# Expert routing stage of a two-layer transformer kernel: the expert choice ahead of the rows' low halves, and a ring of five PSUM banks for gate and up products

## The reference

```python
    def _L0_ffn_ref(x, gate_w, w_up, w_down, sg_gate, sg_up, sg_down):
        ...
        logits = xf @ gate_w.T
        topk_logits, topk_idx = jax.lax.top_k(logits, TOP_K)
        topk_w = jax.nn.softmax(topk_logits.astype(jnp.float32), axis=-1).astype(x.dtype)
        comb = jnp.zeros((N, E), x.dtype).at[jnp.arange(N)[:, None], topk_idx].add(topk_w)
        ...
        for e in range(E):
            g = xf @ wg[e].T
            u = xf @ wu[e].T
            y = jax.nn.silu(g) * u @ w_down[e].T
            out = out + comb[:, e:e + 1] * y
        shared = jax.nn.silu(xf @ sg_gate.T) * (xf @ sg_up.T) @ sg_down.T
        return (shared + out).reshape(b, t, d)
    ...
    x = x + _L0_ffn_ref(_layernorm(x, axis=-1), L0_ffn_gate_w, ...)
```

## Time and profile before

| | us |
|---|---|
| median of 3 runs | 2417.37 |
| lowest, highest | 2417.35, 2419.74 |
| the profiled execution, its own time | 2425.1 |
| its span in the profile | 2423.4 |
| TensorE matmul busy | 2185.1 (90%) |
| VectorE busy | 1776.7 (73%) |
| ScalarE busy | 1664.1 (69%) |
| GpSimd busy | 1076.6 (44%) |

### The profile page before, as it was taken

One profiled execution on the slowest core, in us unless ns is written; L12 is line 12 of the kernel. 1 busy time (PEld: TensorE's weight loads), 2 busy tenths in 40 slices (PEclk: granted clock), 3 DMA queues, 4 the chain that ended last, 5 costly groups with the idle time before them and its releaser, 6 DMA issues. The chain is left out here.

```text
span 2423.4 us, 85735 instructions
## 1 busy us (share of the span) xinstructions
PE 2185.1 (90%) x31693; PEld 1375.4 (57%) x31693; DVE 1776.7 (73%) x5603; ACT 1664.1 (69%) x3894; POOL 1076.6 (44%) x1374
## 2 busy tenths in 40 slices
PE   6979999999967788879999995996999999999766
PEld 4643444444435676768888884563455555555354
DVE  5538999999838677744454444984999999999298
ACT  6955899899843555424454443893799999999644
POOL 3533666666654566636666664562000000000076
PEclk9987999999979899989999998997899999999888
DMA  6552333333232566745553344874232222322242
GB/s 220 203 189 75 93 91 94 94 94 93 65 97 87 146 181 185 171 115 128 141 139 96 93 89 127 267 274 147 65 80 79 81 75 81 82 74 69 64 155 95
DMA packets 363746, 290.45 MB, mean 120 GB/s; under 512 B 228400, under 2 KB 296752, under 8 KB 363344
## 3 DMA queue, kind: packets, MB, share of 16 engines
q1 hardware_dynamic: 349616, 248.24, 37.0%
q0 software_dynamic: 12960, 35.60, 4.7%
q10 hardware_dynamic: 768, 1.12, 0.2%
HBM read 133.53 MB, written 123.69 MB: 106 GB/s over the span
## 5 line engine op out<-in xcount | busy, mean ns | idle before, releaser
L765 ACT ACTIVATE a_pr<-a_pst 128x384 f32<-128x384 f32 (+3 forms) x2176 | 909.2, 486 | 112.6 <-PE a_pst L804 87.3
L804 PE MATMUL a_psc<-a_ke,a_qe 52*64 52x192 f16 (+4 forms) x6144 | 632.4, 286 | 32.5 <-DMA a_ke<-mrow 29.7
L804 PE MATMUL a_pst<-a_qe,a_ke 49*64 49x384 f16 (+5 forms) x6144 | 579.4, 288 | 1.6 <-ACT a_pr L765 0.5
L717 DVE TENSOR_REDUCE a_mx<-a_psc 128x1 f32<-128x320 f32 (+1 forms) x1152 | 537.9, 528 | 44.7 <-PE a_psc L804 36.8
L866 PE MATMUL a_po<-a_pr,a_ve 128*17 128x128 f32 (+3 forms) x10496 | 563.5, 303 | 2.0 <-ACT a_pr L765 1.1
L712 DVE CUSTOM_DVE_ANT_0 a_cut<-a_psc,row_mask 128x320 bf16<-128x320 f32 (+1 forms) x1024 | 436.3, 472 | 51.8 <-PE a_psc L804 29.6
L804 PEld LDWEIGHTS a_pst<-a_qe,a_ke 53*64 53x64 f16 (+1 forms) x6144 | 241.3, 105 | 327.9 <-ACT a_pr L765 193.9
L683 POOL TENSOR_SCALAR_AFFINE_SELECT a_pr<-a_pr 128x512 f32<-128x512 f32 x448 | 276.2, 637 | 159.4 <-ACT a_pr L765 159.4
L804 PEld LDWEIGHTS a_psc<-a_ke,a_qe 52*64 52x64 f16 (+1 forms) x6144 | 262.8, 106 | 112.1 <-DVE a_mx L717 36.3
L866 PEld LDWEIGHTS a_po<-a_pr,a_ve 128*17 128x17 f32 x10496 | 193.9, 96 | 181.9 <-issue 50.5
L663 POOL TENSOR_SCALAR a_mneg<-a_mx 128x32 f16<-128x32 f32 x64 | 18.6, 290 | 626.9 <-DVE a_mx L721 584.7
(11 more groups left out here) (242 smaller groups left out, 4168.6 us busy)
## 6 DMA issues: line engine op xcount, KB each, us to landing
a_qe<-qx SPq DMA_DIRECT2D x378, 64.0 KB, 2.7
a_ke<-kx SPq DMA_DIRECT2D x378, 64.0 KB, 2.7
vx<-p_vst SPq DMA_DIRECT2D x32, 544.0 KB, 3.3
a_ve<-vx SPq DMA_DIRECT2D x64, 272.0 KB, 3.0
qx<-p_stg SPq DMA_DIRECT2D x64, 256.0 KB, 3.4
kx<-p_stg SPq DMA_DIRECT2D x64, 256.0 KB, 3.3
ox<-a_ost SPq DMA_DIRECT2D x256, 64.0 KB
x_res<-x SPq DMA_DIRECT2D x16, 512.0 KB, 8.9
```

Of the source, the lines that this page charges most:

```text
L717: dve.tensor_reduce(out.unsqueeze(1), psc[(u * n_s + n) % RING][:, 0:width], AXX, ALU.max)\
L765: act.activation(pr[s % SLOTS][:, h // 2, h % 2, 0:width], pst[prob_slot(u, n) % RING][:, 0:width], ACT.Exp, scale=scale).then_inc(p_ready, 1)
L804: last = pe.matmul(out[at, col:col + count], stat[:, t * P + 64 * half:t * P + 64 * half + 64], mov[:, tok:tok + count], start=(k == 0), s ...
```

## The change

Two things are changed, both in `stage_route`.

The first is VectorE's order: `top2(s+1)` (or the table, in the last step) now stands ahead of `row_lo(s+2)`.

The second is where gate and up products lie. `pgu` has UR = 5 banks in place of 3, and piece n = 3(2s + h) + f of all pieces goes to bank n mod 5. With the two banks of down products and the small one for logits and ranks all eight banks of PSUM are taken. `up` waits until `hidden` has read the piece five before, not three before. The semaphores `gu_ready`, `gate_done` and `hid_done` are one each now, counted in pieces. Two waits are new, on ScalarE: `silu` waits until `hidden` has read the buffer `gate[f]` it writes (three pieces before), and `high(s, h, f)` until the down product of step s-1 has read `hh[h]`.

```diff
@@ stage_route
+        UR = 5
...
-        pgu = [ctx.enter_context(nc.psum_tensor(f"{tag}_pgu{f}", [P, 2, SL], F32)) for f in range(FC)]
+        pgu = [ctx.enter_context(nc.psum_tensor(f"{tag}_pgu{r}", [P, 2, SL], F32)) for r in range(UR)]
...
+        def piece(s, h, f):
+
+            return FC * (2 * s + h) + f
...
                 if c >= XR:
-                    sp.wait_ge(gu_ready[FC - 1], 2 * (c - XR) + 2)
+                    sp.wait_ge(gu_ready, piece(c - XR, 1, FC - 1) + 1)
...
             def silu(s, h, f):
-                u = 2 * s + h
-                act.wait_ge(gu_ready[f], u + 1)
-                act.activation(gate[:, f, :], pgu[f][:, 0, :], ACT.Silu, scale=PS).then_inc(gate_done[f], 1)
+                n = piece(s, h, f)
+                act.wait_ge(gu_ready, n + 1)
+                after(act, hid_done, n - FC + 1)
+                act.activation(gate[:, f, :], pgu[n % UR][:, 0, :], ACT.Silu, scale=PS).then_inc(gate_done, 1)
 
             def high(s, h, f):
-                u = 2 * s + h
-                act.wait_ge(hid_done[f], u + 1)
+                n = piece(s, h, f)
+                act.wait_ge(hid_done, n + 1)
+                after(act, y_ready[h], s)
...
             def hidden(s, h):
-                u = 2 * s + h
                 for f in range(FC):
-                    dve.wait_ge(gate_done[f], u + 1)
-                    dve.wait_ge(hid_lo[f], u)
-                    dve.scalar_tensor_tensor(out=hid[:, f, :], in0=pgu[f][:, 1, :], scalar=PS * HS,
-                                             in1=gate[:, f, :], op0=ALU.mult, op1=ALU.mult).then_inc(hid_done[f], 1)
+                    n = piece(s, h, f)
+                    dve.wait_ge(gate_done, n + 1)
+                    after(dve, hid_lo[f], 2 * s + h)
+                    dve.scalar_tensor_tensor(out=hid[:, f, :], in0=pgu[n % UR][:, 1, :], scalar=PS * HS,
+                                             in1=gate[:, f, :], op0=ALU.mult, op1=ALU.mult).then_inc(hid_done, 1)
...
                 low(s, 0)
-                if s + 2 < NC:
-                    row_lo(s + 2)
                 if s + 1 < NC:
                     top2(s + 1)
                 else:
                     table_of_tiles()
+                if s + 2 < NC:
+                    row_lo(s + 2)
                 hidden(s, 1)
...
             def up(s, h):
-                u, r, cols = 2 * s + h, s % XR, slice(h * SL, (h + 1) * SL)
+                r, cols = s % XR, slice(h * SL, (h + 1) * SL)
                 for f in range(FC):
-                    pe.wait_ge(hid_done[f], u)
+                    k = piece(s, h, f)
+                    after(pe, hid_done, k - UR + 1)
```

More of the change, by code:

```diff
@@ L1180, in stage_route @@
         scattered = [epoch.also(s) for s in scattered]
-        gu_ready = [sem(f"gu_ready{f}") for f in range(FC)]
-        gate_done = [sem(f"gate_done{f}") for f in range(FC)]
-        hid_done = [sem(f"hid_done{f}") for f in range(FC)]
+        gu_ready, gate_done, hid_done = sem("gu_ready"), sem("gate_done"), sem("hid_done")
         hid_hi = [sem(f"hid_hi{f}") for f in range(FC)]
@@ L1269, in low @@
                 pool.wait_ge(hid_hi[0], 2 * s + h + 1)
-                pool.tensor_tensor(hl[:, h, 0, :], hid[:, 0, :], hh[:, h, 0, :], ALU.subtract).then_inc(hid_lo[0], 1)
+                pool.tensor_tensor(hl[:, h, 0, :], hid[:, 0, :], hh[:, h, 0, :], ALU.subtract)\
+                    .then_inc(hid_lo[0], 1)
             for s in range(NC):
@@ L1408, in low @@
                     dve.wait_ge(hid_hi[f], 2 * s + h + 1)
-                    dve.tensor_tensor(hl[:, h, f, :], hid[:, f, :], hh[:, h, f, :], ALU.subtract).then_inc(hid_lo[f], 1)
+                    dve.tensor_tensor(hl[:, h, f, :], hid[:, f, :], hh[:, h, f, :], ALU.subtract)\
+                       .then_inc(hid_lo[f], 1)
             def add_y(s, h):
@@ L1535, in up @@
             def up(s, h):
-                u, r, cols = 2 * s + h, s % XR, slice(h * SL, (h + 1) * SL)
+                r, cols = s % XR, slice(h * SL, (h + 1) * SL)
                 for f in range(FC):
-                    pe.wait_ge(hid_done[f], u)
+                    k = piece(s, h, f)
+                    after(pe, hid_done, k - UR + 1)
                     for n, f0 in ((0, f * P), (1, F + f * P)):
-                        last = split3(pe, pgu[f][:, n, :], lambda a: ew.uh[:, E, a, f0:f0 + P],
+                        last = split3(pe, pgu[k % UR][:, n, :], lambda a: ew.uh[:, E, a, f0:f0 + P],
                                       lambda a: ew.ul[:, E, a, f0:f0 + P], lambda a: xt[:, r, a, cols],
                                       lambda a: xt[:, r, EC + a, cols], range(EC))
-                    last.then_inc(gu_ready[f], 1)
+                    last.then_inc(gu_ready, 1)
             def down(s, h):
```

## The result

| | before | after |
|---|---|---|
| median of 4 runs each, us | 2418.34 | 2398.88 |
| lowest, highest | 2417.35, 2419.74 | 2394.92, 2399.55 |
| ratio, 95% interval | | 0.9916 [0.9902, 0.993] |
| the profiled execution, its own time | 2425.1 | 2399.03 |
| its span | 2423.4 | 2397.3 |

The change saves 19.5 us, 0.8%. That is inside the range (2380 to 2405) and 11 us above the forecast of 2388, but it is outside the 2381 to 2393 that went with the forecast's own mechanism: the range holds it because it was drawn wide enough for the first rival. It is the time that this rival, "late signals", named, so the time alone doesn't say which mechanism was at work. The trace does.

A forecast was written before the change was run, and what follows sets the result against it. VectorE's chain plus a 2.35 us wait a step for ScalarE's high half was taken as the bound. Savings of 25.7, 1.7, 0.7 and 1.5, sum 29.6 us, from 2417.4 gave 2388 us (2381 to 2393); range 2380 to 2405.

The forecast's parts named there:

- late signals: Rival, gate stage: TensorE's logit signals reach VectorE about 2.2 us late, steps 13.9 to 14.8 us, about 2398 us; chance 0.29.
- The bound: Gate stage: VectorE's chain plus 2.35 us a step waiting for ScalarE's high half sets the 15.84 us step; TensorE follows.
- The order: VectorE: `top2`, 2.64 us long, moves over the idle stretch, T+2.87 to T+5.51 (T: start of `hidden(s, 0)`); step 13.5 us.
- The low halves: VectorE's row low halves beside GpSimd's subtraction: none of the 0.5 us lengthening credited, no change for the next scatter.
- What follows takes 6.33 us.: VectorE from `hidden(s, 1)` to the next `hidden(s+1, 0)`: stays 6.33 us, so its chain allows steps of 13.0 to 13.5 us.
- The sum: Whole gate stage: eleven steps 25.7 us, two other steps 1.7 and 0.7, step 0 1.5; 29.6 us saved, bounds 25 and 36.
- Transposes, ring, new waits: SyncE transposes priced nothing, at most 0.3 us a step; five-bank ring 0, bounds 0 and 0.54; ScalarE's new waits free.
- GpSimd as the bound: Rival: scatters lengthened beside VectorE's moved work delay GpSimd's `low(s, 1)` to T+14.0 to T+15.5; about 2407 us; chance 0.10.
- Slower: Rival: VectorE stands at late logits with low halves queued behind; at T+6.2 a step is 1.0 us longer, 2430; chance 0.07.

The follow-up runs named there:

- before_again: The kernel before, unchanged, profiled once more: 173.93 us for the eleven steps, route 229.80 us, 2415.64 us (one run).
- pool_low_first: The changed kernel with GpSimd's subtraction of half 0 moved ahead of all eight scatters of the chunk, work the same: 2394.80 us, ratio 0.9887.

## Why the prediction was right, and where a term was off

**The bound.** Right. VectorE's loop with its 2.35 us wait set the step, the wait is gone, and TensorE followed: it waits for VectorE at down products and not before `up(s+1, 0)`. One sign that I had named did not come: TensorE is busy 0.91 of the stretch (141.42 of 155.58), not above 0.95, since the step is 14.2 us and not 13.5.

**The order.** The mechanism was right: `top2` fills the idle stretch from T+2.78 (named: T+2.87), and the low halves follow without a wait. The size was off. The failed step is the sentence "It takes 905.86 − 903.22 = 2.64 us, so it runs from T+2.87 to T+5.51, over the idle stretch". The 2.64 us were read where no subtraction of GpSimd stood beside `top2`. The prediction itself had that subtraction at T+5.17 to T+5.86, so the end of `top2` lay in it, but asked only what it would do to the low halves. `top2` measured 3.48 us, 0.84 more.

**The low halves.** Between its bounds: I credited none of the 0.5 us and kept it as the lower bound; all of it came back, as `top2`, lengthened, had taken the overlap upon itself. The next scatter is 0.98 us instead of 1.79, which I had put at no change; it cost nothing before and gives nothing now. Taken together, `hidden(s, 1)` is at T+7.39 where T+6.66 to T+7.16 was named.

**"What follows takes 6.33 us."** Off by 0.46: 6.79. This is the same oversight a second time. The second subtraction had stood beside the two weight halves (1.38 us long). With the step closed up it stands beside the second weight half and reaches the low halves, 1.22 instead of 0.75 us. 7.39 + 6.79 = 14.18 is the step of 14.20, above the upper bound of 13.9.

**The sum.** Named 25.7 + 1.7 + 0.7 + 1.5 = 29.6. Measured against the same profile: 174.20 − 155.58 = 18.6 for the eleven steps, 1.7 (13.52 against 15.22), 0.7 (13.53 against 14.20), 0.5 in step 0, and 2.2 in step 14, which I hadn't counted and which is partly the late signal of that one execution. That is 23.6 (232.17 − 208.53), and 21.3 against before_again. The median gained 19.5. The 29.6 weren't out of reach: without the subtraction on GpSimd the same edit gives 27.7 to 29.0. That the measured time lay in the range was in part luck: the forecast's own bounds for the step, 13.0 to 13.9, missed 14.20, and what the range had beyond 2393 was there for late signals, which did not come.

**Transposes, ring, new waits.** All priced at nothing, rightly. TensorE's wait for transposed rows was 0.2 us in the eleven steps; the ring measured nothing clear of the spread of the recordings three times, in the old order, in the new one, and with TensorE as the bound. Its upper bound of 0.54 us a step was never reached: where the bank is waited for, VectorE's low halves are waited for just behind it.

**The rivals.** *Late signals*: the time came out as named, the mechanism did not; no logit waits in the steady steps, and its cause was absent from every later profile. *GpSimd as the bound*: not in the changed kernel, where scatters kept 0.97 us in the mean and `hidden` never waited for it. My reason against it, that `top2` "is many small operations", was the wrong one, since two of those small operations were lengthened most. That wait is near, as pool_low_first showed. *Slower*: didn't occur; it needed the late signal.

The sentence on the Trainium skill (SBUF — State Buffer, SBUF: two separate sides) was held against the low halves alone. The rule names any VectorE instruction with two SBUF inputs, and `g_hit` agrees with it: begun 0.17 us into GpSimd's subtraction, it ends 0.06 us after it (901.84 + 0.58 against 901.67 + 0.69). `g_hot` does not, by the recorded times. By the rule the one that starts first has the ports, and `g_hot` starts 0.64 us before the subtraction, yet it was held; the measurement decides. Nor would the rule, asked of every instruction of `top2`, have given the missing 0.84 us. These two stand in the kernel before at

```profile
904.98 0.23 DVE L1373 TENSOR_TENSOR g_hot<-g_iota,g_posf 128x64 f32<-128x64 f32 x1
905.24 0.19 DVE L1377 TENSOR_TENSOR g_hit<-g_hot 128x32 f16<-128x32 f32 x1
```

which is 1.76 and 2.02 us into `top2`. With `top2` from T+2.87 they would be over at T+4.86 and T+5.08, before the subtraction at T+5.17. Only a margin of 0.4 us ahead of GpSimd's recorded start, which no run had shown by then, puts both inside it.

## What to carry to other kernels

A duration belongs to its neighbours on the other engines as much as to its instruction: when an edit moves work, list what will stand beside it, and price each small instruction there too. Two subtractions a step, of 0.7 us each when nothing holds them, on an engine with room to spare made the step 1.2 us longer; doing them on the busy engine, at 0.42 us each, was cheaper. And a time that agrees with a forecast proves no mechanism: here 2398.88 us lies in what two rivals named, late signals (2393 to 2405) and GpSimd as the bound (2398 to 2413), and neither reason was the one that held.

## What the runs showed of the hardware

**What GpSimd's subtraction does to small VectorE instructions.** `g_hot` (128x64, two SBUF inputs) goes from 230 to 777 ns, `g_hit` (128x32) from 197 to 585, a cast of 8 columns from 0.17 to 0.63 us (one step of pool_low_first). The instruction under way is held as well as the one that follows: `g_hot` starts at 901.03 and would have ended at 901.26, and GpSimd's instruction is recorded from 901.67, but `g_hot` ends at 901.80; the cast starts at 908.88, the subtraction at 909.44, and the cast ends at 909.51. By their usual lengths both would have ended before GpSimd's instruction is recorded to start, and both end 0.07 to 0.13 us after that. It is so in every steady step: `g_hot` starts 0.62 to 0.68 us before the record in the changed kernel and ends 0.11 to 0.13 us after its start. So whatever holds it begins about 0.4 us or more before that record. Whether the record is late or the hold early stays open. The two instructions together lost 0.55 + 0.39 = 0.94 us to a subtraction of 0.69. Not every neighbour is held: `g_place`, which has one of its two inputs in PSUM, keeps its 0.18 us in pool_low_first where it starts together with the subtraction, and the reduction `g_slotf` its 0.22 us in the changed kernel 0.15 us into one. `g_picked`, with both inputs in SBUF, starts 0.2 us into one in pool_low_first and takes 0.56 us where 0.22 is usual. The cast is held though it reads one tile.

**The same subtraction is itself 0.69 us or 1.37 us long**, the longer where it starts inside a long VectorE instruction (907.39, inside the weights' 906.72 + 1.51; these take 0.95 us alone). Both sides lose there. Where it starts just ahead of a long one it stays at 0.69 us and only the other is longer: 901.52 against 901.57 in the kernel before, 1.73 us and not the 1.22 of the changed kernel.

**Signals of matmuls came late in one recording** (2.16 us behind the recorded end in step 14); neither the second profile of the same kernel nor any of the eleven others has a wait ended by "remote" in this stage. A wait that only one recording shows is best looked for in a second before it carries a rival of 0.29.
